# Half sums of the up and gate weights on GpSimd, and a transposed form of the last pair's denominators

## The reference

```python
# layer 1, feed-forward: the transform can be moved into the weights
x = fwht(x * SU_ug) / SCALE                       # 256-point Hadamard transform
x_up   = x @ W_up.T   * (Wscale_ug[:INTER] * SCALE)
x_gate = x @ W_gate.T * (Wscale_ug[INTER:] * SCALE)
x = fwht(silu(x_gate) * x_up * SU_dp) / SCALE
y = x @ W_down.T * (Wscale_dp * SCALE)
# layer 1, attention
probs = softmax(q @ k.T / 4)
out = (probs @ v) @ out_w.T + out_b               # softmax: divided by its sum
```

## Time and profile before

| | |
|---|---|
| median of 3 runs | 768.29 us (767.82 to 768.45) |
| the profiled execution | 768.83 us, of which the profile's span is 767.0 us |
| PE busy | 707.8 us, 92% |
| DVE, ACT, POOL busy | 552.6, 435.5, 289.2 us |
| mean granted clock of PE | 0.968 of full speed |

### The profile page before, as it was taken

One profiled execution on the slowest core, in us unless ns is written; L12 is line 12 of the kernel. 1 busy time (PEld: TensorE's weight loads), 2 busy tenths in 40 slices (PEclk: granted clock), 3 DMA queues, 4 the chain that ended last, 5 costly groups with the idle time before them and its releaser, 6 DMA issues.

```text
span 767.0 us, 10975 instructions
## 1 busy us (share of the span) xinstructions
PE 707.8 (92%) x4190; PEld 442.0 (58%) x4190; DVE 552.6 (72%) x896; ACT 435.5 (57%) x579; POOL 289.2 (38%) x273
## 2 busy tenths in 40 slices
PE   3778898978997989999999998999999999999997
PEld 3666797957565778867767675333333433333344
DVE  4897766676567756767878888888888288988416
ACT  2542223344443634243242324999999899999883
POOL 0147766432425675254344442012234213423510
PEclk7798999998999999999999999999999999999999
DMA  6126101000202555242211110344334344433321
GB/s 250 55 102 242 56 1 56 1 1 0 102 9 83 161 165 195 83 139 90 77 56 56 55 47 27 124 140 141 112 117 139 93 163 161 136 107 92 100 76 56
DMA packets 25705, 74.14 MB, mean 97 GB/s; under 512 B 4605, under 2 KB 5981, under 8 KB 24693
## 3 DMA queue, kind: packets, MB, share of 16 engines
q1 hardware_dynamic: 21124, 65.37, 25.2%
q0 software_dynamic: 3808, 7.60, 3.3%
q10 hardware_dynamic: 720, 0.48, 0.2%
HBM read 54.54 MB, written 23.06 MB: 101 GB/s over the span
## 4 chain that ended last, share of the span: by engine, by line
PE 58%; DVE 3%; POOL 2%; ACT 2%; issue 1%; DMA 1%; SPq 0%; DVEq 0%; ACTq 0%; POOLq 0%
PE PS L1006 16%; PE PS L742 12%; PE PS L992 11%; PE PS L748 8%; PE PS L975 6%; PE PS L965 4%; DVE mx L1286 1%; DMA scr_k<-spl 1%; POOL sg L1559 1%; ACT P L1473 1%; POOL rot L1579 0%; POOL rot L1580 0%; DVE OE L1333 0%; PE PS L981 0%; ACT spl L1455 0%
## 5 line engine op out<-in xcount | busy, mean ns | idle before, releaser
L1473 ACT ACTIVATE P<-PS 128x1024 f32<-128x1024 f32 x256 | 249.1, 1023 | 30.9 <-PE PS L992 30.6
L1293 DVE TENSOR_REDUCE mx<-PS 128x1 f32<-128x512 f32 x300 | 189.1, 682 | 33.2 <-PE PS L975 31.5
L1286 DVE TENSOR_REDUCE mx<-PS 128x2 f32<-128x1024 f32 x106 | 124.8, 1220 | 37.4 <-PE PS L965 37.1
L1550 POOL TENSOR_TENSOR hl<-sg,hh 128x512 fp32r<-128x512 f32 x64 | 83.5, 1305 | 149.3 <-ACT hh L1435 83.1
L1006 PE MATMUL PS<-P,VV 128*32 128x512 f32 x1024 | 137.2, 608 | 0.1
L992 PEld LDWEIGHTS PS<-QS,KS 64*128 64x128 f32 x512 | 48.6, 183 | 124.0 <-ACT P L1473 110.9
L992 PE MATMUL PS<-QS,KS 64*128 64x512 f32 x512 | 117.1, 457 | 2.3 <-DVE mx L1286 1.8
L975 PE MATMUL PS<-KM,QM 64*128 64x512 f32 x300 | 81.7, 398 | 0.0
L1429 ACT ACTIVATE sg<-PS,cols 128x512 f32<-128x512 f32 x32 | 22.0, 689 | 80.4 <-PE PS L742 80.4
L1559 POOL TENSOR_TENSOR sg<-sg,us 128x512 f32<-128x512 f32 x32 | 42.1, 1316 | 39.4 <-ACT us L1438 39.4
L742 PE MATMUL PS<-XH,UGH 128*128 128x512 f32 x128 | 54.6, 426 | 2.1 <-ACT sg L1429 1.1
(11 more groups left out here) (201 smaller groups left out, 1396.5 us busy)
## 6 DMA issues: line engine op xcount, KB each, us to landing
QM<-scr_q SPq DMA_DIRECT2D x16, 512.0 KB, 4.3
KM<-scr_k SPq DMA_DIRECT2D x16, 512.0 KB, 5.3
QS<-scr_q SPq DMA_DIRECT2D x16, 512.0 KB, 4.4
KS<-scr_k SPq DMA_DIRECT2D x16, 512.0 KB, 5.1
scr_q<-spl SPq DMA_DIRECT2D x24, 256.0 KB, 3.3
scr_k<-spl SPq DMA_DIRECT2D x24, 256.0 KB, 3.5
scr_o<-OE POOLq DMA_DIRECT2D x14, 256.0 KB, 2.8
stg<-in_tern SPq DMA_DIRECT2D x3, 1024.0 KB, 4.8
```

The lines of the kernel that those rows point to most:

```text
L1286: e.tensor_reduce(mx[p % 2][:, :, qt, half], PS[:, b:b + 2, :], AX.X, ALU.max).then_inc(q["mx"], 2)
L1293: e.tensor_reduce(mx[p % 2][:, h, qt, half:half + 1], bank[b], AX.X, ALU.max).then_inc(q["mx"], 1)
L1473: e.activation(P[s % 4][:, half * 1024:(half + 1) * 1024], PS[:, b:b + 2, :].rearrange("p b n -> p (b n)"), ACT.Exp).then_inc(q["ex"], 1)
L1550: e.tensor_tensor(hl[f % 4][:, :], sg[f % 3][:, :], r32(hh[f % 4][:, :]), ALU.subtract).then_inc(q["hl"], 1)
```

## The change

It has two parts.

First, a new piece `halves_ug(n)` on POOL (n = 0 for up, 1 for gate) makes the difference of the two halves of the weights in a new buffer `DIF[n]`, and then their sum in place. `prep_ug` then needs one product for each unit instead of two, and the matrix `HADN` goes. The first unit of each four waits for POOL through the semaphore `hs`. The wait of `signs` for a group of loads moves to its first user, and two waits protect the reused buffers.

Second, `last` is written anew: four products with `OE[1]` as the stationary operand and four columns of `SEL` as the moving one give the 128x16 denominators with tokens on the rows; DVE takes the reciprocal of these 16 columns, copies each 32 times into `RB` (128x512), and four products with the identity `IDN` turn that back; DVE multiplies from PSUM. The six-matmul groups of the projection (`others`) stand around these steps.

```diff
@@ work_order
+            if q == 1:
+                put("halves_ug", 0)
             if q == 2:
                 put("low_attn1")
                 put("load_gate")
         for u in range(8):
             put("prep_ug", u, ps.next())
             yield
+            if u == 0:
+                put("halves_ug", 1)
@@ PE, prep_ug
-                e.wait_ge(d[f"st{i}"], value)
-                e.wait_ge(q["sus"], 3)
-                sums(bank[b], [(HAD[:, :], raw[:, 0, hs]), ((HADN if k else HAD)[:, :], raw[:, 1, hs])]).then_inc(q["pu"], 1)
+                if h == 0:
+                    e.wait_ge(q["hs"], 2 * n + 2)
+                e.matmul(bank[b], HAD[:, :], src[:, h * 512:(h + 1) * 512], start=True, stop=True).then_inc(q["pu"], 1)
@@ POOL
+            def halves_ug(n):
+                i, value = STAGE["up" if n == 0 else "gate"]
+                lo, hi = stg[i][:, 0:1024], stg[i][:, 1024:2048]
+                e.wait_ge(d[f"st{i}"], value)
+                if n == 1:
+                    e.wait_ge(q["pd"], 4)
+                e.tensor_tensor(DIF[n][:, :], lo, hi, ALU.subtract).then_inc(q["hs"], 1)
+                e.wait_ge(q["hs"], 2 * n + 1)
+                e.tensor_tensor(lo, lo, hi, ALU.add).then_inc(q["hs"], 1)
@@ PE, last
+                e.wait_ge(q["gl"], 4)
+                others(0)
+                claim(den)
+                e.wait_ge(d["wl"], 32)
+                for t in range(4):
+                    if t % 2 == 0:
+                        e.wait_ge(q["lo"], t // 2 + 1)
+                    o = e.matmul(bank[den][:, 4 * t:4 * t + 4], OE[1][:, t * 128:(t + 1) * 128], SEL[:, 0:128:32], start=True, stop=True)
+                o.then_inc(q["lden"], 1)
+                others(1)
...
+                e.wait_ge(q["lr"], 2)
+                for t in range(4):
+                    ts = slice(t * 128, (t + 1) * 128)
+                    o = e.matmul(bank[wide_den[t // 2]][:, ts], RB[:, ts], IDN[:, :], start=True, stop=True)
...
+                others(2)
+                others(3)
@@ DVE, last
...
+                e.reciprocal(RL[:, :], bank[den][:, 0:16]).then_inc(q["lr"], 1)
+                e.wait_ge(q["lr"], 1)
+                e.tensor_copy(RB[:, :].rearrange("p (c o) -> p c o", o=32), RL[:, :].rearrange("p (c o) -> p c o", o=1).broadcast_to([128, 16, 32])).then_inc(q["lr"], 1)
```

More of the change, by code:

```diff
@@ L407, in work_order @@
             if t == 8 * NP - 1:
-                put("last", list(range(6)))
+                put("last", [1, 2, 3, 4, 5, 6, 0])
             elif t % 8 == 7:
@@ L486, in program @@
         stg2 = sb("stg2", 190, [128, 2048])
+        DIF = [sb(f"DIF{i}", (198, 190)[i], [128, 1024]) for i in range(2)]
         OB = sb("OB", 202, [128, 256])
@@ L1022, in last, with others @@
                 halves = [slice(0, 256), slice(256, 512)]
[L1023 to L1031, removed]
+                den, *wide_den = banks[:3]
+                acc = banks[3:]
+                def others(n):
+                    claim(acc[n])
                     for r in range(2):
                         ts = slice((2 * n + r) * 128, (2 * n + r + 1) * 128)
-                        two_tiles(bank[b], r, ((OH[1][:, ts], WOH[:, 1, :]), (OH[1][:, ts], WOL[:, 1, :]), (OL[1][:, ts], WOH[:, 1, :])), True, False)
+                        two_tiles(bank[acc[n]], r, ((OH[1][:, ts], WOH[:, 1, :]), (OH[1][:, ts], WOL[:, 1, :]), (OL[1][:, ts], WOH[:, 1, :])), True, False)
+                e.wait_ge(q["gl"], 4)
[8 more added lines that the diff above has]
+                others(1)
+                for b in wide_den:
+                    claim(b)
+                e.wait_ge(q["lr"], 2)
+                for t in range(4):
+                    ts = slice(t * 128, (t + 1) * 128)
+                    o = e.matmul(bank[wide_den[t // 2]][:, ts], RB[:, ts], IDN[:, :], start=True, stop=True)
+                    if t % 2 == 1:
+                        o.then_inc(q["lb"], 1)
+                others(2)
+                others(3)
                 e.wait_ge(q["wl"], 2)
@@ L1087, in ln_norm @@
                 e.wait_ge(q["lnr"], n + 1)
+                if n == 6:
+                    e.wait_ge(q["pu"], 4)
                 if n == 7:
@@ L1112, in signs @@
                 e.tensor_scalar(s16b[:, :], cols[:, z:z + 8], 1.0 / 32, None, ALU.mult).then_inc(q["sus"], 1)
-                e.tensor_scalar(HADN[:, :], HAD[:, :], -1.0, None, ALU.mult).then_inc(q["sus"], 1)
             def tern_scale(n, b):
@@ L1155, in kv_in @@
                 j = tt % 4
+                if tt == 0:
+                    e.wait_ge(d["c"], 48)
                 e.wait_ge(q["kvp"], tt + 1)
@@ L1328, in last @@
                 halves = [slice(0, 256), slice(256, 512)]
[L1329 to L1335 removed]
+                den, *wide_den = banks[:3]
+                acc = banks[3:]
+                e.wait_ge(q["lden"], 1)
+                e.reciprocal(RL[:, :], bank[den][:, 0:16]).then_inc(q["lr"], 1)
+                e.wait_ge(q["lr"], 1)
+                e.tensor_copy(RB[:, :].rearrange("p (c o) -> p c o", o=32), RL[:, :].rearrange("p (c o) -> p c o", o=1).broadcast_to([128, 16, 32])).then_inc(q["lr"], 1)
+                e.wait_ge(d["late0"], 16)
+                for i, qs in enumerate(halves):
+                    e.wait_ge(q["lb"], i + 1)
+                    e.tensor_tensor(OE[0][:, qs], bank[wide_den[i]][:, qs], OE[1][:, qs], ALU.mult).then_inc(q["ln"], 1)
+                for i, qs in enumerate(halves):
                     e.wait_ge(q["lh"], i + 1)
@@ L1620, in low @@
                     e.wait_ge(q["fill"], 2)
-            parts = {f.__name__: f for f in (bias, fold, kv_in, q0, butterfly, low_attn1, up, hidden, ones_v, qk_join, load_wl, out, recip, times, high, low)}
+            parts = {f.__name__: f for f in (bias, fold, kv_in, q0, butterfly, low_attn1, halves_ug, up, hidden, ones_v, qk_join, load_wl, out, recip, times, high, low)}
             for name, *args in order:
```

22 lines of the change are left out of this document (8 added, 14 removed).

## The result

| | before | after |
|---|---|---|
| median, us | 768.37 (767.82 to 768.52, 4 runs) | 771.90 (771.74 to 772.41, 4 runs) |
| profiled execution, its span, us | 768.83, 767.0 | 771.74, 769.9 |

The change makes the kernel slower: the ratio is 1.0048, interval 1.0031 to 1.0066. The prediction was 774.0 us with a range of 771.8 to 776.4.

What follows compares the result with a forecast made beforehand. PE was taken to bound the `prep_ug` stretch. Profiled 768.83 + 6.7 local loss - 1.0 gained at the end = 774.5 us; less 0.54 for the median, 774.0 us, 0.7% slower, range 771.8 to 776.4.

Steps and rivals of the forecast that it cites:

- A with its best end: Rival, PE's clock stays full in units 4 to 7: 773.0 us, 772.6 with end gain 1.4; chance 0.15.
- D: Rival, dearer: narrow passes cost 0.24 us, or the half clock lasts longer or recurs: 776.3 us; chance 0.10.
- the 2.1 of the wide passes: Kernel's end: narrow passes costing as much as 256-column ones add 2.1 us, making the end 1.1 us slower.
- What PE saves is not gained: `prep_ug`: eight products dropped save PE 6.9 us, the whole prize only if nothing waits; PE waits for POOL instead.
- The chain on GpSimd: Halves of up, low parts, gate load, halves of gate: load issued at 209.35, landed at 214.35, unit 4 at 219.35.
- The first wait hidden in the second: PE's 4.9 us before unit 0 vanish in its 4.8 to 6.5 us wait before unit 4, set by POOL's chain.
- The half clock: Behind the wait ahead of unit 4, PE runs 3.4 us at half speed, costing 1.7 us of work.
- The loop of ACT and DVE: From unit 4 it becomes the bound, some 3.6 us per part; first `rot` at 231.3, local loss 6.7 us.
- I carry the loss over whole: Behind `rot`: nothing found tied to an earlier time, so the local loss of 6.7 us reaches the kernel's end.
- rival B: Delay taken up later, by idle time waiting for something like a transfer that does not move: 767.3 us; chance 0.07.
- The end: Last pair's new form: PE's last product starts 1.15 us earlier, counted as a gain of 1.0 us.
- The 0.54 us that I took off for the median: The earlier profiled execution, 768.83, lay 0.54 us above the median of 768.29; 774.5 thus became 774.0 us.

Runs made afterwards that it cites:

- All early: The whole change with the halves of up made earlier in GpSimd's idle time, low parts and gate load two steps earlier: 761.28 us, ratio 0.9885 to the kernel before.
- up early: The whole change with the halves of up made some 26 us earlier, where GpSimd was idle: 767.52 us, ratio 0.9982 to the kernel before.
- PE kept busy: The whole change plus throw-away products on PE while it waits ahead of units 0 and 4: 772.45 us median.
- Part 2 alone: Only the last pair's new form, on the kernel before, with the halves still made by PE: 767.34 us, ratio 0.9966 to the kernel before.

## Why the prediction was right, and where its sizes were off

The direction and the mechanism came out as forecast; that the time lies in the range is in part luck. 771.9 is 0.1 us above its lower end of 771.8, and the lowest case worked out for it, A with its best end, was 772.6: the last 0.8 us had no term behind them. What brought the time down there was not on the list. At the other end D's 776.3 is 0.2 more than 774.0 with the 2.1 of the wide passes.

- **What PE saves is not gained: right.** All of it was lost with two waits for GpSimd. "All early" shows that the prize was real, 5.6 us of 6.9, and that only the place on GpSimd stood in its way.
- **The chain on GpSimd: right to 0.1 us.** Predicted: first wait 4.9, load issued at 209.35 and landed at 214.35, unit 4 at 219.35. Measured: 4.73, 209.19, 214.3 and 219.28. The instructions took 2.34 to 2.38 instead of 2.40.
- **The first wait hidden in the second: right**, and still it was not free, because it pushed the load: "up early" took it away and gained 4.5 us at `rot`.
- **The half clock: right in kind.** Behind unit 0 it lasted twice the 3.4 us assumed (from 203.3 to 210.1), which changed nothing, since PE then waited for unit 4 anyway. Behind unit 4 it lasted 3.4 us, and "PE kept busy" gives its price as 1.0; I had 1.1.
- **The loop of ACT and DVE: right as the bound, 0.6 us too large.** At the full clock I had 10.9 us from unit 4 to `rot`; "PE kept busy" took 10.24. That makes the local loss 6.07 instead of 6.7.
- **"I carry the loss over whole": the step that failed.** 1.9 us came back at one landing. It isn't what rival B meant, a transfer tied to an earlier time: the store was issued 6.07 us later, and its notice came sooner behind the data. "Part 2 alone" has nearly the same early notice (3.98) with no loss to take up, so it is no effect of the delay. The prediction looked only at the transfers that the program issues; what it left out is a packet of instructions, which in the kernel before stood in front of the store's last 4 bytes and in the changed kernel did not. Of the 1.9 us it accounts for 0.9; another 0.7 is the longer time from the last 4 bytes to the landing.
- **The end: right.** 1.18 us by the rows and 1.3 by what lies behind the last copy, 1.15 worked out, 1.0 counted. The narrow products took 0.95 for eight passes, the copy 0.43, near the lower end of my 0.35 to 0.69.
- The sum of these for the profiled execution: 774.5 - 0.6 - 1.9 - 0.2 = 771.8 us; it took 771.74. The 0.54 us that I took off for the median did not repeat: here the median (771.90) is 0.16 above the profiled execution.

**The engine's price or its place?** The Trainium skill, "GPSIMD Engine Reference", section 4.1 (Engine selection), says to keep elementwise work off GpSimd because it is about half as fast with two inputs. Its ratio agrees with the earlier trace rows, but the time does not follow from it: with the same instructions at 2.35 us each, placed in two stretches of idle time (the low parts and the load earlier with them), the kernel has a ratio of 0.9885 to the one before (with the 1.2 us of the end in it); placed in front of a load it has 1.0048.

## What to carry to other kernels

Before moving work to an idle engine, look at what stands behind the new place in that engine's list: here a load, five microseconds from issue to landing, whose data had to come back to the same engine. A dependency that runs engine, load, engine, consumer is one chain, and its last member decides; a wait that is hidden by a later one still costs if it delays the issue of that load. Then search the same list for idle time earlier: two shifts in the order of the work, and nothing else, turned 3.5 us lost into the fastest kernel of the study. And when a shift does not arrive whole, look also at the packets that the program did not ask for.

## What the runs showed of the hardware that I had not expected

- The notice of a store can come late though its data are through. The same 256 KB took 5.56 to 5.81 us from issue to landing in three profiles of one kernel, in which a 16 KB packet of instructions (0.95 to 0.96 us) stood between the data and the last 4 bytes, and 3.52 to 3.98 us in eleven profiles of others. It repeated with the program, not with the time at which the store was issued.
- The half clock can lie on a busy PE: the kernel before was at a mean of 0.57 while PE was busy 3.88 of 4 us. But it came behind a gap, 4 us in which PE was busy 1.96 us at full clock; the fall at 284 us came behind 3 us with 0.95 us busy. The low stretches are 3.4 us of half clock, which is 1.7 us of work, or twice that, and come in some executions of a kernel and not in others (131 to 135 us in one of two profiles of the changed kernel). The two rows:

```profile
471.00:475.00 4.00, 1.96 (x11) 0.78 (x9) 3.91 (x5) 1.98 (x3) 0.00 (x0) 1.00 0.28 86
475.00:479.00 4.00, 3.88 (x17) 1.35 (x17) 3.22 (x6) 2.92 (x4) 1.89 (x2) 0.57 0.00 0
```

- An earlier start can be paid back at the clock: in "part 2 alone" the 1.8 us won at the landing (PE's products at 286.38 instead of 288.18) had become 0.2 by 291.7 us.
